# First and last expert tiles in attention's idle buffers and banks, with a row-halved second product

## What is computed

```python
x = x + 0.5 * ffn(layernorm(x))
x = x + attn(layernorm(x))      # 16 heads of 16, ALiBi; 8 heads look back, 8 ahead; softmax; @ Wf + bf
x = x + 0.5 * ffn(layernorm(x))
def ffn(t):                     # per token
    out = sum over 2 shared experts (width 128): (silu(t @ wg_s) * (t @ wu_s)) @ wd_s
    w, idx = top_k(softmax(t @ router_w), 2); w = w / (sum(w) + 1e-9)
    return out + sum over the 2 chosen of 16 experts (width 64): w * ((silu(t @ wg_r) * (t @ wu_r)) @ wd_r)
```

## Time and profile before

| what | us |
|---|---|
| median of three runs | 2431.34 (2420.27 to 2434.01) |
| profiled execution, its time | 2442.57 |
| profiled execution, its span | 2440.8 |
| PE busy in the span | 1838.3 (75%) |
| DVE, ACT, POOL busy | 1411.0, 1017.9, 940.8 |
| mean granted PE clock | 0.845 |
| DMA moved | 376.46 MB, mean 154 GB/s |
| load of one sequence's x, issue to landing (median) | 4.9 |

### The profile page before, as it was taken

How to read it: one execution, slowest core, us unless ns; L and a number is a source line. 1 busy time by engine, 2 the same in 40 slices (tenths; PEclk the granted TensorE clock), 3 DMA queues, 4 the chain that set the end, 5 groups by cost and what they waited for, 6 DMA issues and landing times.

```text
span 2440.8 us, 34106 instructions
## 1 busy us (share of the span) xinstructions
PE 1838.3 (75%) x10516; PEld 1217.7 (50%) x10516; DVE 1411.0 (58%) x3675; ACT 1017.9 (42%) x2015; POOL 940.8 (39%) x999
## 2 busy tenths in 40 slices
PE   4568885577889888878779777876888898845770
PEld 3455664354656565545445444544655565523550
DVE  5454445657655555567678777775565655563332
ACT  2224442244444444535445444543454554521330
POOL 3432325643432322153554455444233221254416
PEclk8777897888979898978899889988898998976685
DMA  6346663634775566644463546358475656449875
GB/s 181 110 139 210 186 211 125 132 87 96 215 189 150 159 160 176 151 129 86 94 135 88 89 106 134 84 94 257 126 184 142 190 148 155 142 128 300 269 256 155
DMA packets 313027, 376.46 MB, mean 154 GB/s; under 512 B 39304, under 2 KB 256008, under 8 KB 312840
## 3 DMA queue, kind: packets, MB, share of 16 engines
q1 hardware_dynamic: 276880, 289.84, 45.6%
q0 software_dynamic: 24576, 67.14, 10.0%
q10 hardware_dynamic: 11392, 17.31, 2.3%
HBM read 180.71 MB, written 146.80 MB: 134 GB/s over the span
## 4 chain that ended last, share of the span: by engine, by line
PE 45%; DVE 14%; DMA 13%; issue 9%; SPq 8%; another core or an unknown queue 4%; POOL 4%; ACT 2%; ACTq 0%; POOLq 0%; DVEq 0%
PE bank L986 7%; DMA den<-o_store 6%; PE bank L977 6%; PE bank L870 4%; PE bank L1080 4%; PE bank L872 4%; PE bank L871 4%; PE bank L1060 4%; PE bank L1027 3%; PE bank L1093 3%; PE bank L967 2%; SPq L818 2%; DVE den L1525 2%; DVE row_max L1428 2%
## 5 line engine op out<-in xcount | busy, mean ns | idle before, releaser
L1428 DVE TENSOR_REDUCE row_max<-bank 128x1 f32<-128x512 f32 (+2 forms) x768 | 349.2, 504 | 188.9 <-PE bank L1043 121.9
L1206 ACT ACTIVATE p_buf<-bank 128x512 f32<-128x512 f32 x640 | 361.3, 596 | 223.9 <-PE bank L1060 134.0
L1639 POOL TENSOR_SCALAR_AFFINE_SELECT p_buf<-p_buf 128x512 f32<-128x512 f32 x256 | 160.8, 642 | 420.8 <-ACT p_buf L1206 420.1
L1027 PE MATMUL bank<-k_stack,q_stack 99*128 99x512 bf16 (+3 forms) x1024 | 258.5, 323 | 78.3 <-issue 48.9
L1583 POOL DMA_INDIRECT sorted_x<-xn,position x256 | 250.4, 978 | 107.3 <-issue 69.5
L1060 PE MATMUL bank<-q_stack,k_stack 101*128 101x512 bf16 (+3 forms) x1024 | 244.6, 316 | 62.3 <-issue 18.3
L1605 POOL DMA_INDIRECT y_tok<-sorted_y,position x216 | 206.4, 956 | 192.0 <-DVE x_ffn L1495 65.1
L986 PE MATMUL bank<-t_w,t_h 64*128 64x256 f32 x752 | 244.4, 451 | 41.9 <-DVE t_h L1482 30.4
L977 PE MATMUL bank<-t_xt,t_w 128*128 128x256 f32 x752 | 237.3, 444 | 48.1 <-DMA t_w<-expert_w 32.6
L1080 PE MATMUL bank<-p_buf,v_rows 128*32 128x512 f32 (+3 forms) x2048 | 197.6, 488 | 15.0 <-POOL p_buf L1639 10.4
L986 PEld LDWEIGHTS bank<-t_w,t_h 64*128 64x128 f32 x752 | 142.7, 210 | 118.7 <-DVE t_h L1482 50.6
(11 more groups left out here) (165 smaller groups left out, 3591.4 us busy)
## 6 DMA issues: line engine op xcount, KB each, us to landing
t_w<-expert_w SPq DMA_DIRECT2D x188, 256.0 KB
t_x<-sorted_x SPq DMA_DIRECT2D x188, 256.0 KB
sorted_y<-t_y SPq DMA_DIRECT2D x188, 256.0 KB
q_stack<-qk_part SPq DMA_DIRECT2D x192, 128.0 KB
k_stack<-qk_part SPq DMA_DIRECT2D x192, 128.0 KB
sorted_x<-zeros SPq DMA_DIRECT2D x68, 256.0 KB, 3.6
o_store<-o_raw ACTq DMA_DIRECT2D x64, 256.0 KB
x_ffn<-in_L_attn_x SPq DMA_DIRECT2D x16, 512.0 KB, 4.9
```

Source lines behind the costliest of these rows:

```text
L1027: pe.matmul(ps[:, col:col + k1 - k0], q_stack[0:ROWS_S, h, P * qt:P * qt + P], k_stack[0:ROWS_S, h, k0:k1], start=(n == 0), stop=False, sk ...
L1206: act.activation(p_of(u), psum("score", *of)[:, :], ACT.Exp).then_inc(*exp_done.step(*of))
L1428: ins = dve.tensor_reduce(row_max[g % 2][:, n:n + 1], src[:, col:col + q1 - q0], X, ALU.max)
```

## The change

- `GROUPS`: the second layer's groups are sequences 0 to 11 and 12 to 15. Tiles: 39, 55, 63 and 31.
- "Many tiles" are the first and the last group. Their tiles use `t_x[3..6]` (four, in `p_buf[0]`) and `t_w[3..8]` (six, in `p_buf[1]` and `[2]`), and up to six banks ("wide"), as do the feed-forwards of sequences 0 to 5 in the first layer and of the last one in the second.
- Sequences 2 to 5 of the first layer have x buffers of their own in q_stack and `xn` buffers of their own in k_stack; the constant rows of both stacks are loaded once these are free. Sequences 0 to 5 turn through three `act_t`, the third in `y_tok`; the raw attention weights go to `p_buf[1]`.
- The 16 zero fills of the first and the last group are split between SP and ACT.
- Gathers of the second layer turn through five buffers. The index computation (`find`) doesn't wait for the tiles any more. Gathers of the third group are due later, after the last sequence's feed-forward.
- Second product of all tiles: the hidden tensor lies as two halves, tokens 0 to 127 in partitions 0 to 63 and tokens 128 to 255 in partitions 64 to 127 (the down weights were in both halves of `t_w` already). The two matmuls use rows 0 to 63 and 64 to 127 of the array and write to two banks; two ACT copies of 256 columns take the place of one of 512; the second DVE operation is two of 128 columns, through a new `t_g`.

```diff
-GROUPS = (((0, 6), (6, 16)), ((0, 11), (11, 16)))
+GROUPS = (((0, 6), (6, 16)), ((0, 12), (12, 16)))
...
-BANKS = {"row": 3, "score": 2, "out": 1, "fill": 3}
+BANKS = {"row": 3, "score": 2, "out": 1, "fill": 3, "wide": 6}
+EARLY = range(2, min(6, GROUPS[0][0][1]))
+def many_tiles(l, g):
+    return (l, g) in (ALL_GROUPS[0], ALL_GROUPS[-1])
+def first_buffer(b):
+    return b if b in EARLY else b % 2
 def norm_buffer(kind, l, b):
-    return 1 if kind == "att" else b % 2 if l == 0 else 0
+    return 1 if kind == "att" else first_buffer(b) if l == 0 else 0
 def act_buffer(kind, l, b):
-    return 0 if kind == "att" else b % 2 if l == 0 else 1
+    return 0 if kind == "att" else 1 if l else b % 3 if b < GROUPS[0][0][1] else b % 2
 def y_buffer(l, b):
-    return 1 + (b - LAST) % 4 if l == 1 and b >= LAST else 0
+    return b % 5 if l == 1 else 0
...
+    def fill(kind, l, b):
+        return "wide" if kind == "ffn" and (l == 0 and b < GROUPS[0][0][1] or l == 1 and b == B - 1) else "fill"
...
-        part(at + 1.0 * pace, "PE", 1.1, made, (hidden, "DVE"), takes=[
-            bank("fill", ("ty", l, g, j), (made, "ACT"))], lag=0.3)
+        part(at + 1.0 * pace, "PE", 0.65, made, (hidden, "DVE"), takes=[
+            bank(fill, ("ty", l, g, j, t), (made, "ACT")) for t in range(2)], lag=0.3)
...
-        part(at, "DVE", 1.15, gather, (("table", l, g), "DVE"), (("position", l, b), "POOL"), *made)
+        part(at - 1.0, "DVE", 1.15, gather, (("table", l, g), "DVE"), (("position", l, b), "POOL landed"))
...
-        part(at + 0.1, "SP", 13.0, ("fill", l, g), (("table", l, g), "DVE"), *old, lag=4.0)
+        if many_tiles(l, g):
+            part(at + 0.1, "SP", 10.4, ("fill", l, g), (("table", l, g), "DVE"), *old, lag=4.0)
+            part(at + 0.1, "ACT", 10.4, ("fill", l, g), (("table", l, g), "DVE"), *old, lag=4.0)
+        else:
+            part(at + 0.1, "SP", 20.8, ("fill", l, g), (("table", l, g), "DVE"), *old, lag=4.0)
...
+            if not many_tiles(1, g):
+                at = max(at, start + 16 * (B + 1) + 12.6 + 0.1 * b)
             gathering(at, 1, b)
...
-        t_x = [sb(f"t_x{i}", [P, 2, D]) for i in range(3)]
-        t_w = [sb(f"t_w{i}", [P, ND * P + D]) for i in range(3)]
+        t_x = [sb(f"t_x{i}", [P, 2, D]) for i in range(3)] + [
+            p_buf[0][:, i, :].rearrange("p (t d) -> p t d", d=D) for i in range(4)]
+        t_w = [sb(f"t_w{i}", [P, ND * P + D]) for i in range(3)] + [p_buf[c][:, i, :] for c, n in ((1, 4), (2, 2))
+                                                                     for i in range(n)]
-        t_h = [sb(f"t_h{i}", [ME, RT]) for i in range(2)]
+        t_g = sb("t_g", [ME, RT])
+        t_h = [sb(f"t_h{i}", [P, RT // 2]) for i in range(2)]
...
+        for flat, of in ((q_flat, x_ffn), (k_flat, xn)):
+            of += [flat.bitcast(F32)[:, NT * D * i:NT * D * (i + 1)].rearrange("p (t d) -> p t d", d=D)
+                   for i in range(4)]
...
                 elif name == "stack rows":
+                    for b in EARLY:
+                        sp.wait_ge(*x_put[0, b].at(b))
+                        sp.wait_ge(*sent[b].at(0, b, 2 * NT - 1))
+                        for d in range(ND):
+                            sp.wait_ge(*xt_full.at("ffn", 0, b, d))
...
                 elif name == "tile out":
-                    for t in range(2):
-                        ins = pe.matmul(ps[:, D * t:D * t + D], hidden[:, P * t:P * t + P],
-                                        weights[0:ME, ND * P:ND * P + D], start=(t == 0), stop=(t == 1),
-                                        skip_group_check=True)
+                    halves = [take(("ty", *of, t), ty_out, *of, t) for t in range(2)]
+                    for t in range(2):
+                        at = slice(ME * t, ME * t + ME)
+                        ins = pe.matmul(halves[t][:, 0:D], hidden[at, :], weights[at, ND * P:ND * P + D],
+                                        start=True, stop=True)
...
-                    dve.tensor_tensor(t_h[i][:, :], ps[ME:P, 0:RT], t_h[i][:, :], ALU.mult
-                                      ).then_inc(*th_step.step(*of, "u"))
+                    for t in range(2):
+                        at = slice(P * t, P * t + P)
+                        dve.tensor_tensor(t_h[i][ME * t:ME * t + ME, :], ps[ME:P, at], t_g[:, at], ALU.mult
+                                          ).then_inc(*th_step.step(*of, "u", t))
```

More of the change, by code:

```diff
@@ L162, in place @@
                 mine[:] = [freed for freed in mine if not finished(freed)]
-                if len(mine) >= self.limit(use):
+                if len(mine) + sum(what == kind for _, what, _, _ in got) >= self.limit(use):
                     return None
@@ L167, in place @@
                     old = tenant.get(("bank", i))
+                    if any(home == ("bank", i) for home, _, _, _ in got):
+                        continue
                     if old is None or finished(old[1]):
@@ L266, in transposes @@
             piece = "transpose", kind, l, b, d
-            takes = [bank("fill", ("xt", kind, l, b, d), (piece, "DVE"))]
+            takes = [bank(fill(kind, l, b), ("xt", kind, l, b, d), (piece, "DVE"))]
             if d == 0:
@@ L308, in shared @@
             part(at[4 + half], "PE", 1.65, down, *[(("split", l, b, j), "POOL") for j in range(NSH)],
-                 takes=[bank("fill", ("y", l, b, half), (down, "DVE"))], lag=0.3)
+                 takes=[bank(fill("ffn", l, b), ("y", l, b, half), (down, "DVE"))], lag=0.3)
             part(at[4 + half], "DVE", 0.69, down, (down, "PE"))
@@ L317, in tile @@
         sent = [(("position", l, b), "POOL") for b in range(*GROUPS[l][g])]
-        part(at - 2.5, "SP", 0.8, x, (("fill", l, g), "SP"), *sent,
-             takes=[("t_x", ("t_x", l, g, j), [(flip, "PE")])], lag=4.0)
-        part(at - 2.5, "SP", 0.9, weights, (("table", l, g), "DVE"), (("expert weights",), "SP"),
-             takes=[("t_w", ("t_w", l, g, j), [(made, "PE")])], lag=4.0)
+        fills = [(("fill", l, g), "SP")] + ([(("fill", l, g), "ACT")] if many_tiles(l, g) else [])
+        last = [(("values", B - 1, NG - 1, 2), "PE")] if (l, g) == ALL_GROUPS[-1] else \
+            [(("attention weights",), "DVE")] if (l, g) == ALL_GROUPS[0] else []
@@ L322, in tile @@
+        part(at - 2.5, "SP", 0.8, x, *fills, *sent, *last,
+             takes=[("wide_x" if many_tiles(l, g) else "t_x", ("t_x", l, g, j), [(flip, "PE")])], lag=4.5)
+        part(at - (4.0 if many_tiles(l, g) else 2.5), "SP", 0.9, weights, (("table", l, g), "DVE"),
+             (("expert weights",), "SP"), *last,
+             takes=[("wide_w" if many_tiles(l, g) else "t_w", ("t_w", l, g, j), [(made, "PE")])], lag=4.5)
+        fill = "wide" if many_tiles(l, g) else "fill"
         part(at, "PE", 0.65, flip, (x, "SP"), takes=[
-            bank("fill", ("tx", l, g, j), (flip, "ACT")), ("t_xt", ("t_xt", l, g, j), [(hidden, "PE")])], lag=0.3)
+            bank(fill, ("tx", l, g, j), (flip, "ACT")), ("t_xt", ("t_xt", l, g, j), [(hidden, "PE")])], lag=0.3)
@@ L332, in tile @@
-        part(at + 1.0 * pace, "ACT", 0.6, made, (made, "PE"),
+            bank(fill, ("tgu", l, g, j), (hidden, "DVE")), ("t_h", ("t_h", l, g, j), [(made, "PE")])], lag=0.3)
+        part(at + 0.6 * pace, "ACT", 0.38, hidden, (hidden, "PE"),
+             takes=[("t_th", ("t_th", l, g, j), [(hidden, "DVE")])])
+        part(at + 0.6 * pace, "DVE", 0.98, hidden, (hidden, "ACT"))
+        part(at + 1.0 * pace, "PE", 0.65, made, (hidden, "DVE"), takes=[
+            bank(fill, ("ty", l, g, j, t), (made, "ACT")) for t in range(2)], lag=0.3)
@@ L333, in tile @@
+        part(at + 1.0 * pace, "ACT", 0.8, made, (made, "PE"),
              takes=[("t_y", ("t_y", l, g, j), [(put, "SP landed")])])
@@ L359, in schedule @@
     part(20.3, "DVE", 0.45, ("bias",), (("bias",), "PE"))
-    part(20.4, "SP", 2.0, ("stack rows",), lag=4.0)
+    part(8 * GROUPS[0][0][1], "SP", 2.0, ("stack rows",), *[(("put", 0, b), "SP landed") for b in EARLY],
+         *[(("position", 0, b), "POOL landed") for b in EARLY], lag=4.0)
     def feed_forward(g, begin, step, tiles_from, pace):
@@ L524, in build @@
         y_tok = sb("y_tok", [P, 2, NT, D])
[L526 removed]
+        act_t = [sb(f"act_t{i}", [P, 2, ND, S], F32R) for i in range(2)] + [
+            y_tok[:, :, :, :].rearrange("p c t d -> p c (t d)").rearrange("p c (k s) -> p c k s", k=ND).bitcast(F32R)]
         q_stack = sb("q_stack", [P, H, S], BF16)
@@ L743, in do @@
                     sp.wait_ge(*table_step.at(l, g, "fill"))
-                    for e in range(E):
+                    for e in range(0, E, 2 if many_tiles(l, g) else 1):
                         row = sp.value_load(fill_i[0:1, e:e + 1])
```

138 lines of the change are left out of this document (84 added, 54 removed).

## The result

The changed kernel took 2307.1 us, median of four runs (2305.0 to 2316.8), where the kernel before took 2425.8 in the same session: a ratio of 0.9525, 95% interval 0.9467 to 0.9584. A second session gave 0.948 (0.9446 to 0.9514), 2299.1 against 2425.3. So it is 4.7 to 5.2% faster, 119 to 126 us; 154 were forecast, and 2277 us in place of 2307.

A forecast was written before the change was run, and what follows sets the result against it. TensorE was taken as the bound from 198 to 2145 us, except 1060 to 1670, with waits and DMA at the ends. Savings 32 + 7 + 26 + 22 + 12 + 55 = 154 us took 2431.3 to 2277; range 2215 to 2350.

The forecast's parts named there:

- Own buffers, -32: Feed-forward of sequences 2 to 5: early x loads cut 27 us a sequence to 19, saving 32 us.
- Fills, -7: Before the first tile: splitting zero fills over SP and ACT leaves SP eight fewer, saving 7 us.
- Row halves, 0.49 us a tile: Tile's second product: halves on different array rows run 1.6 times as fast, 1.30 to 0.81 us of PE.
- Halves one after the other: Rival, 10%: the second product gains nothing from row halves; 70 us less gain, 2347 us.
- Program order: Rival, 8%: the second product's records need three slots of four, 0.33 us a tile; 25 us less gain, 2302.
- First tiles, -26: Tile stretch 198 to 400 us: 39 tiles save 19 us, more weight and x buffers perhaps 7; 26 us.
- Second group, -12: Tiles inside attention, 640 to 1060 us: 55 tiles save 27 us, taken as 22 for shared banks.
- Slower: Rival, 4%: tiles in attention wait for two of three banks at once, 1.6 us each; 2500 us.
- Third group, -12: Third group, 63 tiles starting one sequence later: tiles save 19 us, one tile-free sequence costs 7; 12 us saved.
- Tail, -55: After attention: -18 to the first tile (-8 from later gathers), -27 for DMA-bound late tiles, -10 for fewer last gathers.
- Held by the queue: Rival, 12%: in the tail, SP's outputs waiting for a combine hold the next weights; the -27 goes, 2304 us.
- The front: Rival, 8%: one h_buf and one POOL queue keep early sequences at 27 us each; 32 us less gain, 2309.

The follow-up runs named there:

- one-bank product: Changed kernel with the row-halved second product undone: one bank, one ACT copy, one DVE multiply; ratio 0.9757 to the kernel before.
- landing waits: Changed kernel, but in the last layer POOL waits after each sequence's eight gathers until they have landed; ratio 0.9503 to the kernel before.
- two buffers: Changed kernel with two gather buffers instead of five in the last layer; ratio 0.947 to the kernel before.

## Why the prediction came out as it did

The verdict, faster, and the range held; 154 us were forecast and 119 to 135 came. But that the sum came so near is luck, two errors that offset each other: 47 us too little up to the end of attention, 66 too much after it.

*Own buffers, -32.* Half right. The pace is as forecast: sequence 1 to 5 in 77 us, 19.3 each, 31 us less than before. The start took 15 of them back: position of sequence 0 at 49.5 instead of 39.4, of sequence 5 at 144.1 instead of near 128. The step that failed is "with the loads early": their place in SP's queue, behind the expert weights, was not looked up, nor what stands behind DVE's wait for them. Moving the loads gave sequence 5 at 131.4.

*Fills, -7.* From position of sequence 5 to the first tile's copy 28.8 us instead of 29.9: 1. Eight fills still take SP 12.0 us where sixteen took 17.1, 1.5 each for 1.1, and begin 6.1 us after the position instead of 3.8. The term took the cost of a fill as fixed.

*Row halves, 0.49 us a tile.* Measured 0.52. With a granted clock of 1.0 a tile's four records take 0.70 us, where they took 1.13:

```profile
2375.77 1.13 PE L986 MATMUL bank<-t_w,t_h 64*128 64x256 f32 x4 [0.32 <-DVE t_h L1482]
```

```profile
2086.86 0.70 PE L1064 MATMUL bank<-p_buf,t_h 64*128 64x256 f32 x4
```

That refutes two rivals. Halves one after the other would have left 1.13. Program order would give three slots of four, 0.85. In the trace the four records start in pairs: at 0, 0.01, 0.32 and 0.33 us (medians over 148 tiles at full clock), where before they started at 0, 0.32, 0.54 and 0.75. That is two slots for four; it is 0.70 and not half of 1.13 because the last record's own length, 0.38 us, stands at the end of both. The section of the Trainium skill quoted in the prediction ("TensorE: Matmul & The Clock Gate", part 3) isn't refuted by this, since the records do keep one order in start and end. What failed is the step from it to three slots; which half a record belongs to, no row tells.

*First tiles, -26.* First to last tile 160 us instead of 193: -33. Three banks in place of six took 9 of these back and the one-bank product 19 (179 us there). That the rest comes from the transfers' buffers is argued; no run undoes these. *Second group, -22.* From sequence 0 to 11 -45. A tile costs 1.0 us less, not 0.4. That would be 55 us; sequence 5, the first without tiles, gives some back, 93.9 us to the next first mask where it was 83.1. With the one-bank product it costs 2.8 (172 row matmuls and 49 tiles in 640 to 1000), so 0.2 come from elsewhere and 0.8 from the product, more than its own 0.52: DVE's and ACT's added halves cost nothing there, and banks hardly ran short: PE waits 7.8 us in four waits for a bank that ACT's second-product copies free, 0.15 us a tile where the rival *Slower* put 1.6. That the rest is a product that ends sooner and frees its bank sooner is argued, not shown.

*Third group, -12.* -50 from sequence 11 to the end of attention. It is the same saving for a tile, and eleven tiles that were put off behind attention. That is no gain but a debt that the tail pays. The forecast's "+15 to -30" for this group did not ask where the last tiles would run.

*Tail, -55.* +11. This is the step that failed. Attention's end to the first late tile, 79.8 us before, took 73.9: -6 for -18. The -8 for gathers ahead of the chain was wrong: the last sequence's scatters begin 50 us after attention's end with them (2192.6) and 49 without them (2045.8). The fills gave the rest, 12.1 us for 20.9, of which 3.9 went because SP begins them 4.4 us after the first scatter and not 0.5. Late tiles, first transpose to last product, 154 us before, took 180: +25 for -27. The rest, 64 us before, took 56: -8 for -10. The second is the large one. "DMA is the bound: 42.6/325 = 131 us" assumed a share near 1.00; it was 0.74, with 0.54 in the long run of gathers. The rate itself was right: with the landing waits the DMA engines gave 318 GB/s at 0.98. Sign and size of "gathers that now flow faster" were wrong: the first 48 flow in place of the tiles. And the -27 would not have reached the end: with the landing waits the tiles had it, and the time was the same.

That is because of a sum that I had not made. POOL has 128 gathers behind attention's end. From start to start one takes 1.28 us where POOL waits for nothing (1.30 by the earlier trace rows), 164 us in all, and the first now starts at 2080.0, 83 us after the end of attention (2 us before). 83 + 164 + 9 for the last combine and store are 256 us, and the forecast left 298 - 55 = 243. With 53 us of waits on top it is the 309 measured. The last 32 gathers begin between 2246 and 2256 in the changed kernel, with two buffers, with landing waits and with three banks, though the last tile is taken over at 2235, 2203, 2181 and 2242: gathers and POOL's own waits (52 to 54 us in the first three; 72 with three banks, 35 of them in one) fill the time. The waits that POOL has in this chain in the changed kernel:

```profile
POOL q_stack L1705 <- DVE x_ffn L1595: 23.3, 2, 13.5
...
POOL y_tok L1705 <- DVE x_ffn L1595: 16.3, 2, 16.0
...
POOL k_stack L1705 <- DVE x_ffn L1595: 13.5, 1, 13.5
```

53 us in five waits for combines. That these are late because they stand in DVE's queue behind tile steps is argued. The five buffers put off the waiting of the earlier trace rows (65.1 us) and didn't remove it.

*The rivals.* Held by the queue: SP's wait for the second product in the tail did vanish (0.2 us for 34.9), and the -27 failed for another reason; the time it gave, 2304, was nearly met without its mechanism. The front did not stay chained. Of the prediction's own signs three came (four records in 0.70 us that start in pairs, no wait of SP, 32 gathers at the end) and three did not (sequence 5 near 128, a DMA share over 0.9 between the late tiles, no gather waiting for a combine).

## What to carry to other kernels

Add up each engine's own queue behind the point where the bound ends, with the time its first item can start: that floor (here POOL's 128 gathers) can decide before the bandwidth does. When tiles are moved past the end of a stretch, book them where they land. And when a wait is removed, ask what the engine now does without a pause: here a longer unbroken run of indirect transfers took from the tiles what it saved itself.

## What the runs showed of the hardware

Two matmuls of 64 rows on the two halves of the array, each a float32 product of 256 columns with its own bank, took 0.70 us together where the same two on one half took 1.13, a factor of 1.6; their records start in pairs, 0.01 us apart.

Forty of the first 48 indirect transfers of the tail, issued one every 1.25 us without a pause, left two tiles in 49 us, with a quarter of the bytes too, and though each landed within some 6 us; with 3 to 6 us of pause after eight, or one every 2.35 us, 17 tiles ran beside the same forty. Runs of 16 as dense left three or four tiles in 20 us. Which resource they hold isn't shown by any view: the waiting engines stand under "issue", and the DMA engines were busy only 0.27 to 0.54 of the time. The Trainium skill, "DMA: Bandwidth & Descriptors", section on the ways to generate descriptors, says that a DMA engine serves its queues for software and hardware descriptors in turn. The trace doesn't test that: SP itself issued only seven plain transfers in these 49 us. Spacing the forty otherwise than by these ways was not tried.
